# Work ahead of step 0 of a modulated linear and a GRU: block 0's x on its own, the norm first, biases from small loads

## The reference

```python
ys = cond * 256 ** -0.5
d  = rsqrt(einsum('bi,io->bo', ys * ys, W0 * W0) + 1e-8)
x  = x + einsum('bsi,io->bso', x * ys[:, None, :], W0) * d[:, None, :]
Xz, Xr, Xh = (einsum('btc,hc->tbh', x, Wx) + bx for each gate)
def step(H, xs):
    Z = sigmoid(xz + H @ Whz.T + bhz)
    R = sigmoid(xr + H @ Whr.T + bhr)
    H_tilda = tanh(xh + R * H @ Whh.T + bhh)
    H_new = Z * H + (1 - Z) * H_tilda
    return H_new, H_new @ Whq.T + bhq
x = x + outputs of the 256 steps from H = cond
```

## Time and profile before

| | us |
|---|---|
| median of 3 runs | 636.63 (636.57 to 637.08) |
| the profiled execution's own time | 637.65 |
| its span | 635.9 |
| PE busy | 624.7 (98%) |
| DVE busy | 465.4 (73%) |
| ACT busy | 279.5 (44%) |
| POOL busy | 4.5 (1%) |

### The profile page before, as it was taken

One profiled execution on the slowest core, in us unless ns is written; L12 is line 12 of the kernel. 1 busy time (PEld: TensorE's weight loads), 2 busy tenths in 40 slices (PEclk: granted clock), 3 DMA queues, 4 the chain that ended last, 5 costly groups with the idle time before them and its releaser, 6 DMA issues.

```text
span 635.9 us, 40091 instructions
## 1 busy us (share of the span) xinstructions
PE 624.7 (98%) x16890; PEld 566.6 (89%) x16890; DVE 465.4 (73%) x3794; ACT 279.5 (44%) x2119; POOL 4.5 (1%) x11
## 2 busy tenths in 40 slices
PE   8999999999999999999999999999999999999987
PEld 3589999999999999999999999999999999999976
DVE  3888777776777777777777777777677777767776
ACT  2244444444444444444444444444444444444443
POOL 0200000000000000000000000000000000000000
PEclk9955555555555555555555555555555555555555
DMA  7000000000000000000000000000000000000000
GB/s 265 2 4 4 5 12 5 3 13 4 13 4 13 4 5 12 5 12 5 11 6 4 13 4 13 4 5 12 5 12 5 12 5 4 12 4 13 4 12 12
DMA packets 7176, 8.87 MB, mean 14 GB/s; under 512 B 1618, under 2 KB 5458, under 8 KB 6996
## 3 DMA queue, kind: packets, MB, share of 16 engines
q1 hardware_dynamic: 6416, 6.03, 3.0%
q10 hardware_dynamic: 580, 0.28, 0.2%
HBM read 4.21 MB, written 2.10 MB: 10 GB/s over the span
## 4 chain that ended last, share of the span: by engine, by line
PE 93%; DVE 4%; ACT 1%; DMA 1%; issue 1%; DVEq 0%
PE chunk_bank L691 53%; PE z_rec_bank L691 13%; PE chunk_bank L668 12%; PE z_bank L668 6%; PE y_bank L653 6%; PE chunk_bank L700 2%; DMA x<-x_cm 1%; PE chunk_bank L605 1%; DVE lin L404 1%; DVE r_hidden L538 1%; DVE hidden L584 1%; DVE r_hidden L542 0%; DVE r_hidden L546 0%; ACT scan_mul L343 0%; DVE xs L397 0%
## 5 line engine op out<-in xcount | busy, mean ns | idle before, releaser
L691 PE MATMUL chunk_bank<-r_hidden,w_part 128*128 128x8 bf16 x6144 | 206.3, 169 | 0.2
L691 PEld LDWEIGHTS chunk_bank<-r_hidden,w_part 128*128 128x128 bf16 x6144 | 184.7, 105 | 19.5 <-issue 0.6
L343 ACT ACTIVATE scan_mul<-z_pre 128x16 f32<-128x16 f32 x256 | 57.2, 224 | 196.8 <-DVE z_pre L550 196.8
L691 PEld LDWEIGHTS chunk_bank<-hidden,w_part 128*128 128x128 bf16 x3072 | 102.8, 104 | 30.8 <-DVE hidden L584 6.0
L691 PE MATMUL chunk_bank<-hidden,w_part 128*128 128x8 bf16 x3072 | 125.2, 173 | 4.4 <-DVE hidden L584 3.9
L691 PE MATMUL z_rec_bank<-hidden_parts,w_part 128*128 128x24 bf16 x3072 | 121.6, 181 | 0.1
L691 PE MATMUL chunk_bank<-hidden_parts,w_part 128*128 128x8 bf16 x3072 | 117.8, 168 | 0.0
L538 DVE TENSOR_TENSOR r_hidden<-r_bank,hidden 128x8 f32<-128x8 f32 x256 | 42.6, 166 | 97.0 <-ACT r_bank L341 95.3
L691 PEld LDWEIGHTS z_rec_bank<-hidden_parts,w_part 128*128 128x128 bf16 x3072 | 103.3, 104 | 0.2 <-DVE z_rec_bank L486 0.2
L691 PEld LDWEIGHTS chunk_bank<-hidden_parts,w_part 128*128 128x128 bf16 x3072 | 101.5, 104 | 0.0
L584 DVE TENSOR_TENSOR_SCAN hidden<-scan_mul,r_bank 128x24 f32<-128x24 f32 x256 | 52.0, 203 | 58.0 <-ACT r_bank L346 52.2
(11 more groups left out here) (92 smaller groups left out, 801.5 us busy)
## 6 DMA issues: line engine op xcount, KB each, us to landing
x<-x_cm SPq DMA_DIRECT2D x4, 512.0 KB, 8.1
out_cm<-result SPq DMA_DIRECT2D x15, 128.0 KB, 2.2
w_rec<-w_rec_cm SPq DMA_DIRECT2D x1, 768.0 KB, 8.5
w_in<-w_in_cm SPq DMA_DIRECT2D x1, 768.0 KB, 10.2
w_mod<-w_mod_cm ACTq DMA_DIRECT2D x1, 256.0 KB, 5.7
w_out<-w_out_cm SPq DMA_DIRECT2D x1, 256.0 KB, 10.6
out_cm<-result SPq DMA_DIRECT2D x1, 64.0 KB, 2.5
out_cm<-result SPq DMA_DIRECT2D x2, 32.0 KB, 1.9
```

What stands on the lines that cost most here:

```text
L343: nc.scalar.activation(scan_mul[:, :, 2::3], z_pre[:, :, :], ACT.Sigmoid, scale=-1.0)
L691: return nc.tensor.matmul(cols, w_part[wp][:, gate, k, m * P:(m + 1) * P], moving, start=first, stop=True, skip_group_check=True)
```

## The change

It makes five pieces of x in place of four: steps 0 to 15 (block 0), 16 to 63, and three of 64. On TensorE the norm's products come ahead of the linear, the bias products go, and linears 0 to 3 follow one another ahead of block 0's input products; linear 4 stands in step 0, and waits for `lin_ready` 3. Pieces 0 and 1 share the banks `chunk_bank[0]`. The biases come by four loads straight to the partitions, and VectorE sums them. VectorE's order is new, and pieces 2 and 3 are modulated by ScalarE, one activation per chunk and sequence (64 elements each, 32 in all).

```diff
     NB = T // BLOCK
-    GROUPS = 4
-    GC = T * B // GROUPS
+    STEPS = ((0, BLOCK), (BLOCK, T // 4), (T // 4, T // 2), (T // 2, 3 * T // 4), (3 * T // 4, T))
+    PIECES = len(STEPS)
     PARTS = 3
...
-        bias_rows = sb("bias_rows", [2, 2, C])
+        gate_bx_bh = sb("gate_bx_bh", [P, 2, 2, KC])
         ones = sb("ones", [2, 1])
...
-        def lin_bank(i, m):
-
-            return (chunk_bank[0], chunk_bank[1], (y_bank, r_bank), chunk_bank[1])[i][m]
+        def lin_bank(i, m, lo, hi):
+
+            bank = (chunk_bank[0], chunk_bank[0], chunk_bank[1], (y_bank, r_bank), chunk_bank[1])[i][m]
+            at = B * (STEPS[i][0] if i == 1 else 0)
+            return bank[:, at + lo * B:at + hi * B]
...
         ld_zbias = sem("ld_zbias")
-        ld_x = [sem(f"ld_x{i}") for i in range(GROUPS)]
+        ld_x = [sem(f"ld_x{i}") for i in range(PIECES)]
         ld_win, ld_wrec, ld_wout = sem("ld_win"), sem("ld_wrec"), sem("ld_wout")
...
-            return 1 + KC * max(0, n + 1 - NB // GROUPS)
+            return 1 if n == 0 else 2 + KC * max(0, n + 1 - NB // 4)
...
             def load_x(i):
-                at = slice(i * GC, (i + 1) * GC)
+                at = slice(B * STEPS[i][0], B * STEPS[i][1])
                 sp.dma_start(x[:, :, at], x_cm[:, :, at]).then_inc(ld_x[i], 16)
...
             load_x(1)
+            load_x(2)
             sp.dma_start(w_rec[:, :, :, :], w_rec_cm).then_inc(ld_wrec, 16)
-            load_x(2)
+            load_x(3)
             sp.dma_start(w_in[:, :, :, :], w_in_cm).then_inc(ld_win, 16)
-            load_x(3)
+            load_x(4)
             sp.dma_start(w_out[:, :, :], w_out_cm).then_inc(ld_wout, 16)
...
             act.dma_start(w_mod[:, :, :], w_mod_cm).then_inc(ld_wmod, 16)
-            act.dma_start(bias_rows[:, :, :], gate_bias[0:2, :, :]).then_inc(ld_bias, 16)
+            for gate in range(2):
+                for row in range(2):
+                    act.dma_start(gate_bx_bh[:, gate, row, :], gate_bias[row, gate, :].rearrange("(k p) -> p k", p=P),
+                                  allow_slow_non_contiguous=True).then_inc(ld_bias, 16)
             act.dma_start(z_bx_bh[:, :, :], z_bias).then_inc(ld_zbias, 16)
...
             act.wait_ge(wide_ready, 1)
-            act.wait_ge(lin_ready, 1)
+            act.wait_ge(lin_ready, 2)
             for i in range(2 * KC):
                 seed_gate(0, i // KC, i % KC)
+
+            for i in (2, 3):
+                act.wait_ge(linp_ready, i + 1)
+                lo, hi = STEPS[i]
+                for k in range(KC):
+                    for b in range(B):
+                        mul = nc.scalar.activation(
+                            lin[:, k, lo:hi, b], lin_bank(i, k, 0, hi - lo).rearrange("p (t b) -> p t b", b=B)[:, :, b],
+                            ACT.Copy, scale=d[:, k, b:b + 1])
+                mul.then_inc(lin_ready, 1)
             act.wait_ge(z_seeded, 1)
-            act.wait_ge(lin_ready, 3)
+            act.wait_ge(lin_ready, 4)
             feed_scan(0)
...
                     if j == 4:
-                        act.wait_ge(lin_ready, GROUPS)
+                        act.wait_ge(lin_ready, PIECES)
                     seed_gate(1 - p, (j - 4) // KC, j % KC)
...
                 dve.wait_ge(ld_x[i], 16)
-                steps = slice(i * T // GROUPS, (i + 1) * T // GROUPS)
+                lo, hi = STEPS[i]
                 for k in range(KC):
                     nc.vector.tensor_tensor(
-                        xs[:, k, steps, :], x[:, k, i * GC:(i + 1) * GC].rearrange("p (t b) -> p t b", b=B),
-                        ys[:, k, :].unsqueeze(1).to_broadcast([P, T // GROUPS, B]), ALU.mult).then_inc(xs_ready[k], 1)
+                        xs[:, k, lo:hi, :], x[:, k, B * lo:B * hi].rearrange("p (t b) -> p t b", b=B),
+                        ys[:, k, :].unsqueeze(1).to_broadcast([P, hi - lo, B]), ALU.mult).then_inc(xs_ready[k], 1)
...
-                at = i * T // GROUPS
+                at = STEPS[i][0]
                 return nc.vector.tensor_tensor(
-                    lin[:, k, at + lo:at + hi, :], lin_bank(i, k)[:, lo * B:hi * B].rearrange("p (t b) -> p t b", b=B),
+                    lin[:, k, at + lo:at + hi, :], lin_bank(i, k, lo, hi).rearrange("p (t b) -> p t b", b=B),
                     d[:, k, :].unsqueeze(1).to_broadcast([P, hi - lo, B]), ALU.mult)
...
-                dve.wait_ge(linp_ready, i + 1)
-                for k in range(KC):
-                    mul = modulate_steps(i, k, 0, T // GROUPS)
+                dve.wait_ge(linp_ready, 2)
+                for k in range(KC):
+                    mul = modulate_steps(i, k, 0, STEPS[i][1] - STEPS[i][0])
                 mul.then_inc(lin_ready, 1)
...
-            scale_x(0)
             dve.wait_ge(ld_wmod, 16)
             nc.vector.tensor_tensor(w_mod_sq[:, :, :], w_mod[:, :, :], w_mod[:, :, :], ALU.mult).then_inc(wsq_ready, 1)
-            scale_x(1)
-            first_rest(0)
+            scale_x(0)
             dve.wait_ge(dsq_ready, 1)
...
                                     EPS, None, ALU.add).then_inc(d_sq_ready, 1)
-            first_rest(1)
-            dve.wait_ge(bias_summed, 1)
-            nc.vector.tensor_copy(gate_bias_cm[:, :, :], z_bank[:, 0:2 * KC]
-                                  .rearrange("p (g k) -> p g k", g=2)).then_inc(bias_ready, 1)
+            scale_x(1)
+            dve.wait_ge(ld_bias, 64)
+            nc.vector.tensor_tensor(gate_bias_cm[:, :, :], gate_bx_bh[:, :, 0, :], gate_bx_bh[:, :, 1, :], ALU.add
+                                    ).then_inc(bias_ready, 1)
             dve.wait_ge(ld_zbias, 16)
...
             scale_x(2)
+            first_rest(0)
+            dve.wait_ge(d_ready, 1)
+            for i in range(2):
+                modulate(i)
+                dve.wait_ge(lin_ready, i + 1)
+                for k in range(KC):
+                    add = add_x(k, slice(B * STEPS[i][0], B * STEPS[i][1]))
+                add.then_inc(x1_ready, 1)
+            first_rest(1)
+            scale_x(3)
             first_rest(2)
-            second_rest(0)
-            dve.wait_ge(d_ready, 1)
-            modulate(0)
-            dve.wait_ge(lin_ready, 1)
-            for k in range(KC):
-                add = add_x(k, slice(0, GC))
-            add.then_inc(x1_ready, 1)
-            second_rest(1)
-            modulate(1)
-            scale_x(3)
-            second_rest(2)
-            modulate(2)
+            for i in range(3):
+                second_rest(i)
+            scale_x(4)
             dve.wait_ge(in0_ready, 1)
...
                     if j == 0:
-                        dve.wait_ge(linp_ready, GROUPS)
+                        dve.wait_ge(linp_ready, PIECES)
                     for k in range(KC):
-                        mul = modulate_steps(GROUPS - 1, k, j * BLOCK, (j + 1) * BLOCK)
+                        mul = modulate_steps(PIECES - 1, k, j * BLOCK, (j + 1) * BLOCK)
                     if j == 3:
                         mul.then_inc(lin_ready, 1)
-                if NB // GROUPS <= n + 2 < NB:
+                if NB // 4 <= n + 2 < NB:
                     if j == 4:
-                        dve.wait_ge(lin_ready, GROUPS)
+                        dve.wait_ge(lin_ready, PIECES)
                     if j in (4, 5):
...
+                lo, hi = STEPS[i]
                 for k in range(KC):
...
                     for m in range(KC):
-                        mm = nc.tensor.matmul(lin_bank(i, m)[:, :], w_mod[:, k, m * P:(m + 1) * P],
-                                              xs[:, k, i * T // GROUPS:(i + 1) * T // GROUPS, :]
-                                              .rearrange("p t b -> p (t b)"),
-                                              start=(k == 0), stop=True, skip_group_check=True)
+                        mm = nc.tensor.matmul(lin_bank(i, m, 0, hi - lo), w_mod[:, k, m * P:(m + 1) * P],
+                                              xs[:, k, lo:hi, :].rearrange("p t b -> p (t b)"),
+                                              start=(k == 0 and i != 1), stop=True, skip_group_check=True)
                 mm.then_inc(linp_ready, 1)
...
             pe.wait_ge(ld_wmod, 16)
-            lin_tiles(0)
             pe.wait_ge(ys_ready, 1)
...
             mm.then_inc(dsq_ready, 1)
-
-            pe.wait_ge(ld_bias, 16)
-            pe.wait_ge(ones_ready, 1)
-            for gate in range(2):
-                for k in range(KC):
-                    at = gate * KC + k
-                    mm = nc.tensor.matmul(z_bank[:, at:at + 1], bias_rows[:, gate, k * P:(k + 1) * P], ones[:, :],
-                                          start=(at == 0), stop=True, skip_group_check=True)
-            mm.then_inc(bias_summed, 1)
-            lin_tiles(1)
-            lin_tiles(2)
+            for i in range(4):
+                lin_tiles(i)
...
                 if t == 0:
-                    pe.wait_ge(lin_ready, 2)
-                    lin_tiles(GROUPS - 1)
```

(3 more changed lines are left out.)

## The result

The changed kernel takes 641.25 us (median of 4 runs, 640.69 to 641.48) against 636.69 for the kernel before on the same chip: ratio 1.0069, 95% interval 1.0052 to 1.0087, so 4.6 us slower.

What follows compares the result with a forecast made beforehand. 256 successive recurrent steps, with a chain of waits ahead of step 0, bound the kernel. Step 0's candidate products ending at 33.4 instead of 30.74 us added 2.7 to the median 636.63: 639.3 us, range 634.8 to 641.5.

Steps and rivals of the forecast that it cites:

- The sign and the mechanism: Slower (chance 0.62): VectorE waits for four bias loads behind its scaling of piece 1, with later scalings and linears behind that.
- The landing: ScalarE's queue before step 0: biases land at 15.5 us, z bias half a us later, scaling 2 begins at 16.1.
- a count of packets one for one: ScalarE's 1088 small packets alternate with as many of SP's, so the biases are in at 14.5 to 15 us.
- a rate: Small packets move at 71.5 a us until 15.5 us, the rest at the first load's pace: biases in at 17.0.
- Step 0 from there: VectorE's and TensorE's work from scaling 2 on: step 0's candidate products end at 33.4 against 30.74, later by 2.7 us.
- w_mod landed: Load for the early norm: in at 6.2 us (bounds 5 and 6.8), so d is there at about 12, not 18.4.
- ScalarE's activations: ScalarE's modulation before step 0: 32 activations at 0.15 us, 4.8 in all, hidden, with step 0's sigmoids at 29.5.
- rival 3: Bias loads later still (scaling 2 at 22, sum 645), or TensorE at lower clock level from linear 2 (641); chance 0.12.
- the sum: Whole time: the trace's 2.7 us difference at step 0's candidate products, added to the three runs' median of 636.63: 639.3.
- The upper end: Top of the forecast range for the whole time, 641.5 us; some 0.1 of chance is left out on either side.

Runs made afterwards that it cites:

- e2: Changed kernel with the biases laid out on the host and brought by one load instead of four strided ones: 635.58 us.
- e3: Changed kernel, its four strided loads kept, with VectorE's wait for them and the two bias sums moved behind the third first-rest: 637.11 us.
- e6: Kernel before, with one matmul of zeros ahead of the linear in place of 10: 637.50 us, ratio 1.0024.
- e5: Kernel before, with 16 matmuls of zeros ahead of the linear in place of 10: 635.17 us, ratio 0.9987.
- e9: Changed kernel with 16 matmuls of zeros in place of 10: 641.27 us.
- e4: Kernel before with four strided bias loads, the sum on VectorE where the copy stood, and TensorE's eight bias products gone: 638.48 us, ratio 1.0049.
- e11: Kernel before with 16 matmuls of zeros in place of 10, run again on another chip: 635.03 us.

## Why the prediction was right, and where it was off

*The sign and the mechanism held.* The bias loads decide (e2: 5.6 us back), by VectorE's wait (e3: 4.1 of them).

*The landing.* I took 15.5 for the biases and 16.1 for scaling 2, between a count of packets one for one (14.5 to 15) and a rate (17.0); 15.0 and 16.04 were measured. The count was the right one: 1356 to 1365. My 16.1 was nearer than its parts: the biases came 0.5 sooner than I took them, and the z bias 0.75 behind them, not 0.5. Each strided load did make 256 packets and 16 more, as ScalarE's queue carried 1664 in all, and 580 before (1088 new ones, less 4 of the load that they replace). That agrees with the Trainium skill (*DMA: Bandwidth & Descriptors*, rules for kernel authors), by which such a load is lowered to one descriptor per element. The packets under 512 bytes rose by 1102, where I had said 1024. The same page (queues, rings and completion order) also says that an engine drains some 9 to 17 descriptors of a queue before it switches. Equal counts alone do not speak against that, since groups of equal size would give them too. The single packets of the trace do: from 8 to 14 us, 83% of ScalarE's have one of SP's beginning exactly 6 ns after them, against 6 to 21% at every other distance up to 14 ns.

*Step 0 from there.* Forecast 33.4, measured 33.43. Of the pieces, scaling 3's first half was through at 22.1 for 21.8 and linear 3 over at 25.8 for 25.4; block 0's products, linear 4 and the candidate took what the rows said.

*Terms that were off and did not matter here.* w_mod landed at 4.8, not 6.2, outside my bounds of 5 to 6.8, so d came at 11.0 for 12. ScalarE's activations took 0.20 each, not 0.15: 6.7 us from the first to the end of the last, the sigmoids at 31.6, still under linear 4. Once the wait is moved they are on the path (e3). TensorE did fall to the lower level in its wait, as rival 3 had it, and linear 2 took 5.40 in place of 3.5 (rival 3 had 6.8). Busy time by stage in the changed kernel (length, PE, PEld, DVE, ACT, POOL, granted clock, DMA):

```profile
14.00:20.00 6.00, 3.22 (x4) 1.31 (x5) 4.28 (x12) 0.63 (x1) 0.74 (x2) 0.77 0.21 71
20.00:22.00 2.00, 2.00 (x5) 0.72 (x3) 2.00 (x5) 0.51 (x1) 0.00 (x0) 0.85 0.00 0
22.00:24.00 2.00, 2.00 (x6) 0.93 (x6) 2.00 (x5) 0.82 (x3) 0.00 (x0) 1.00 0.00 0
```

The clock goes to 0.77 of full in the mean of the stage with the gap, and is back from 22 us on. Linear 2 ended at 22.2, when scaling 3 had just become ready, and cost 0.1.

*The step that was off most* is the one on which the sum stood: "I take the difference on the trace and add it to the median". The trace of before was of an execution 1.0 us above its median, and not by chance noise: its first linear ran at the lower level, and the bias products behind it released VectorE at 15.8. With the level up sooner that comes 1.5 or 3 us sooner (e6, e5). The changed kernel has no such better executions in its runs, because the loads' landing is not moved by TensorE's level (e9: scaling 2 began at 16.62, though the first linears were at the upper level). So 2.7 us at the end of step 0 is the price against an execution of the kernel before whose first linear is wholly at the lower level, 6.2 against its best band, and 4.6 against its median. I had read the 1061 ns rows and used them as a constant. Of the 1.95 us between forecast and result, 1.0 is this; most of the rest, 0.8, is the steps' pace in the two traces (605.2 and 606.0).

That the result still fell inside the range is partly luck. The upper end was there for a later landing or a lower level (rival 3), and neither is what added the time.

## What to carry to other kernels

Count packets, not bytes, for a small load that shares the DMA engines with big ones: here it moved one packet for one of the other queue's, so that some 1100 packets of 4 bytes, which need 9 ns of an engine each, lasted as long as an equal number of SP's, of up to 6 KB. Lay such an array out on the host, or put the wait where the data are wanted and not where they were written down. Before adding a difference from one trace to a median, ask whether the trace's execution is like the others, above all in a stretch whose durations change with TensorE's level; a start held at one level (e5) gives a measure with 0.4 us of spread in place of 3.6.

## What the runs showed that I had not expected

- After the same ten matmuls of zeros and the same gap the first linear took 6.5 us (the kernel before) or 3.7 (e4), and with a single matmul of zeros 5.1 (e6). The time of the kernel before moves by 3 us in bands. Six more matmuls of zeros (no result depends on them) brought the median down by 1.5 us (e5; e11: 1.6, ratio 0.9970, interval 0.9959 to 0.9982), by taking away its two upper bands: the best runs of the kernel before are as fast.
- The small packets held back the big ones by less than can be told here: w_rec landed 7.8 to 9.6 us after its issue beside them, and 8.3 to 9.0 without, in the traces of all the runs.
- The issue of the z bias, 0.36 us before, took 1.81 behind the four strided loads, so that ScalarE began its table load at 6.5 in place of 3.5. It hid, since w_rec landed at 11.4. In e4 the time was in the four strided issues instead (3.20, and 0.63 for the z bias), and the table load began at 6.1. The timeline of its queue in the changed kernel:

```profile
1.62 2.41 ACTq L302 DMA_DIRECT2D gate_bx_bh<-gate_bias  x4
4.06 1.81 ACTq L304 DMA_DIRECT2D z_bx_bh<-z_bias  x1
5.90 0.61 ACTq L305 DMA_DIRECT2D bq<-out_bias  x1
```
